# Flamingo layer with gated attention and experts, one core: the router's logits from the float16 halves, turned by DMA, instead of TensorE's float32 turns

## What is computed

```python
def reference(x, ctx_1024, g_xattn, g_ffn, ...):                # x and ctx: (8, 512, 512) float32
    x = x + tanh(g_xattn[0]) * xattn(layernorm(x), ctx, ctx, Wq, bq, Wk, bk, Wv, bv, Wo, bo)   # 16 heads of 32
    x = x + tanh(g_ffn[0]) * ffn(layernorm(x), Wr, br, W1, b1, W2, b2)

def ffn(x, Wr, br, W1, b1, W2, b2):
    probs = softmax(x @ Wr + br)            # the router: 4096 tokens, 8 experts
    gates, ids = top_k(probs, 2)
    # each expert takes up to 615 tokens, hidden size 2048, silu, and adds gate * result to its tokens
```

## Time and profile before

| | |
|---|---|
| time, median of 3 runs | 1811.75 us (1811.48 to 1812.64) |
| the profiled execution | 1810.6 us, of which the span is 1808.9 us |
| PE busy | 1727.7 us, 96% of the span |
| DVE, ACT, POOL busy | 60%, 44%, 24% |
| granted clock of PE, mean | 0.981 of full speed |
| attention | up to about 903 us of the span, 8 batches |

### The profile page before, as it was taken

How to read it: one execution, slowest core, us unless ns; L and a number is a source line. 1 busy time by engine, 2 the same in 40 slices (tenths; PEclk the granted TensorE clock), 3 DMA queues, 4 the chain that set the end, 5 groups by cost and what they waited for, 6 DMA issues and landing times.

```text
span 1808.9 us, 29536 instructions
## 1 busy us (share of the span) xinstructions
PE 1727.7 (96%) x10371; PEld 827.7 (46%) x10371; DVE 1076.8 (60%) x2087; ACT 798.2 (44%) x1093; POOL 434.4 (24%) x424
## 2 busy tenths in 40 slices
PE   6999999999999999999918999999999999999998
PEld 4324243342423334243305657475665647565563
DVE  6777867778776777867687625345252525434231
ACT  4553735547364554735423426153342516244240
POOL 2332434224343332431201211211021121112101
PEclk9999999999999999999958999999999999999999
DMA  6334263433425433243123542625263362626312
GB/s 227 106 86 125 71 167 113 102 119 100 144 93 142 137 93 116 81 114 109 42 100 105 133 124 100 168 87 154 71 174 80 120 148 88 179 50 177 75 44 29
DMA packets 214608, 203.19 MB, mean 112 GB/s; under 512 B 121813, under 2 KB 162913, under 8 KB 210457
## 3 DMA queue, kind: packets, MB, share of 16 engines
q1 hardware_dynamic: 193432, 181.80, 33.1%
q0 software_dynamic: 21120, 20.67, 6.6%
HBM read 134.57 MB, written 43.63 MB: 99 GB/s over the span
## 4 chain that ended last, share of the span: by engine, by line
PE 84%; DVE 10%; issue 3%; ACT 2%; POOL 1%; DMA 0%; SPq 0%; DVEq 0%; ACTq 0%; POOLq 0%
PE psum L1598 23%; PE psum L1574 21%; PE psum L1369 7%; PE psum L1376 6%; PE psum L1360 6%; PE psum L1350 6%; PE psum L1340 6%; PE psum L1462 5%; PE psum L1387 3%; DVE mx L938 2%; DVE reached L1092 1%; DVE x2hl L1012 1%; DVE x2hl L1014 1%; DVE stats L890 1%; DVE x2n L897 1%
## 5 line engine op out<-in xcount | busy, mean ns | idle before, releaser
L1598 PE MATMUL psum<-w,hT 128*128 128x512 f16 (+1 forms) x1920 | 415.7, 379 | 0.0
L1574 PE MATMUL psum<-xgT,w 128*128 128x308 f16 (+1 forms) x3072 | 408.1, 293 | 0.6 <-DVE xgT L1193 0.6
L938 DVE TENSOR_REDUCE mx<-psum 128x1 f32<-128x512 f32 x512 | 330.2, 683 | 104.1 <-PE psum L1350 102.5
L1574 PEld LDWEIGHTS psum<-xgT,w 128*128 128x128 f16 x3072 | 296.2, 97 | 109.3 <-DVE xgT L1193 1.1
L788 ACT ACTIVATE pt<-psum 128x1024 f32<-128x1024 f32 x256 | 255.0, 1022 | 116.4 <-PE psum L1360 116.4
L1598 PEld LDWEIGHTS psum<-w,hT 128*128 128x128 f16 (+1 forms) x1920 | 199.3, 104 | 213.8
L864 ACT ACTIVATE h<-psum,b1c 128x308 f32<-128x308 f32 (+1 forms) x256 | 117.9, 511 | 342.0 <-PE psum L1574 341.6
L1214 DVE TENSOR_TENSOR hT<-h,hT 128x615 f16<-128x615 f32 x128 | 102.5, 801 | 210.1 <-ACT hT L867 210.1
L681 POOL DMA_INDIRECT out_dram<-y,idx_now x40 | 87.6, 2191 | 498.8 <-DVE y L1246 305.8
L1243 DVE SCALAR_TENSOR_TENSOR y<-psum,b2b 128x512 f32<-128x512 f32 (+1 forms) x40 | 27.7, 691 | 269.4 <-PE psum L1598 269.4
L1340 PE MATMUL psum<-actT,wT 128*128 128x512 f16 x768 | 177.6, 379 | 2.0 <-DVE wT L925 2.0
(11 more groups left out here) (198 smaller groups left out, 1522.7 us busy)
## 6 DMA issues: line engine op xcount, KB each, us to landing
stage<-in_L_ffn_W_dram SPq DMA_DIRECT2D x62, 1024.0 KB, 5.9
stk<-qk_rows SPq DMA_DIRECT2D x192, 128.0 KB, 2.5
qk_rows<-qks SPq DMA_DIRECT2D x64, 256.0 KB, 2.5
xin<-in_x_dram SPq DMA_DIRECT2D x8, 1024.0 KB, 5.3
cin<-in_ctx_dram SPq DMA_DIRECT2D x8, 1024.0 KB, 7.5
xres<-in_x_dram SPq DMA_DIRECT2D x8, 1024.0 KB, 5.6
out_dram<-xres SPq DMA_DIRECT2D x32, 256.0 KB, 2.1
x_split<-x2hl SPq DMA_DIRECT2D x32, 256.0 KB, 2.3
```

The source lines that it names most:

```text
L938: v.reduce_max(mx[:, KT * t + qt:KT * t + qt + 1], ps, AX.X).then_inc(read, 1)
L1574: mm = t_.matmul(psum[:, (2 * m + ch) % 4, 0:c1 - c0], w1[:, wp, kt, m * P:(m + 1) * P], xgT[:, KT * xp + kt, c0:c1], start=(kt == 0 and ( ...
L1598: mm = t_.matmul(psum[0:rows, Y_BANK[i], :], hT[:, hp, k, c * P:c * P + rows], w2[:, wp, k, :], start=(k == 0 and (hp, wp) == (0, 0)), sto ...
```

## The change

The 16 transposes on PE in slot 2 and ACT's four copies of them are gone. SP turns `x2hl`, the halves that DVE has made already, by four DMA transposes of 128x1024 float16 into `x2T`, a float16 view of `x2nT`; they stand in SP's list behind `stack_heads` of tile 5 and ahead of the maxima of group 0, and only from batch 1 on. `wr` is split into halves once, ahead of the batches. `parts` is now three products for each quarter (high by high, high by low, low by high), 12 float16 products, in the second half of slot 5 ahead of that half's values, and PE waits there for all four transposes. `logits` moves to the second half of slot 6, behind that half's values.

```diff
-X2T_SLOT, PARTS_SLOT, LG_SLOT = 2, 4, 5
+PARTS_SLOT, LG_SLOT = 5, 6
...
+        wr_hl = sb("wr_hl", [P, 2, KT, 32], f16)
...
+        x2T = x2nT[:, :, :].rearrange("p k s -> p (k s)").bitcast(f16).rearrange("p (c s) -> p c s", s=S)
...
                 for i in range(QK_FIRST + 2):
                     stack_heads(sp, b, i)
+                if not first:
+                    sp.wait_ge(x2hl_ready, KT * b)
+                    settle(sp)
+                    for tt in range(KT):
+                        sp.dma_start(x2T[:, :, tt * P:(tt + 1) * P], x2hl[:, tt, :], transpose=True).then_inc(x2T_in, 16)
                 for g in range(NG):
 
                     sp.wait_ge(mrow_ready, NG * b + g + 1)
...
+            s.activation(wr_hl[:, 0, :, :], wr[:, :, :], ACT.Copy, scale=SW).then_inc(wr_hi, 1)
+
+            def logit_parts(b):
+                ps, read = filled(act, use, "lg_parts", b)
+                s.activation(lg_parts[:, :], ps, ACT.Copy, scale=1.0 / SW).then_inc(read, 1)
...
-                    if t == X2T_SLOT:
-                        rows()
                     if t == PARTS_SLOT:
-                        parts()
+                        logit_parts(b)
                     if t < LAG_B:
                         for tt in later_v(t):
                             values(tt)
                     if t == LG_SLOT:
-                        logits()
+                        logits(b)
...
+            dve.wait_ge(wr_hi, 1)
+            v.scalar_tensor_tensor(wr_hl[:, 1, :, :], wr[:, :, :], SW, wr_hl[:, 0, :, :], ALU.mult, ALU.subtract).then_inc(wr_split, 1)
...
+                    if first:
+                        pe.wait_ge(wr_split, 1)
+                    else:
+                        pe.wait_ge(x2T_in, 16 * KT * b)
+                    dst, full = claim(pe, use, "lg_parts", b)
+                    for xp, wp in PARTS:
+                        for kt in range(KT):
+                            last = t_.matmul(dst[32 * kt:32 * kt + 32, :], wr_hl[:, wp, kt, :], x2T[:, KT * xp + kt, :],
+                                             start=((xp, wp) == (0, 0)), stop=((xp, wp) == (1, 0)))
                     last.then_inc(full, 1)
...
-                    if s == X2T_SLOT:
-                        rows((2 * half, 2 * half + 1))
```

More of the change, by code:

```diff
@@ L251, in batch_banks @@
                     banks.add(("qk", i), (2, 4, 2, 4)[i - QK_FIRST])
-                if s == X2T_SLOT:
-                    for kt in range(KT):
-                        banks.add(("x2T", kt), (6, 7, 3, 5)[kt])
                 if s == PARTS_SLOT:
@@ L315, in layer_kernel @@
         settled = sem("settled")
-        wr_zero, pick_ready = sem("wr_zero"), sem("pick_ready")
+        wr_zero, wr_hi, wr_split, x2T_in, pick_ready = (
+            sem(n) for n in ("wr_zero", "wr_hi", "wr_split", "x2T_in", "pick_ready"))
         k_ones = sem("k_ones")
@@ L551, in _ @@
             g.memset(minus_half[:, :], -0.5).then_inc(consts_ready, 1)
-            g.memset(x2n[:, :, :], 0.0).then_inc(consts_ready, 1)
+            g.memset(x2nT[:, :, :], 0.0).then_inc(consts_ready, 1)
             pool.wait_ge(ident_zero, 1)
@@ L717, in _, with logits @@
             copied(act, pre, "bias")
[L719 to L734, removed]
+            s.activation(wr_hl[:, 0, :, :], wr[:, :, :], ACT.Copy, scale=SW).then_inc(wr_hi, 1)
+            def logit_parts(b):
+                ps, read = filled(act, use, "lg_parts", b)
+                s.activation(lg_parts[:, :], ps, ACT.Copy, scale=1.0 / SW).then_inc(read, 1)
+            def logits(b):
+                ps, read = filled(act, use, "lg", b)
+                settle(act)
+                s.activation(lg[:, b, :], ps[:, 0:KT * E], ACT.Copy).then_inc(read, 1)
             def batch(b, last):
-                rows, parts, logits = router_copy(use, b, b)
                 def queries_keys(i):
@@ L1295, in _, with batch @@
                 copied(pe, pre, ("w", 3, kt))
[L1297 to L1303, removed]
-                def parts():
[L1307 to L1312, removed]
+            def batch(b, last_batch, first=False):
+                def parts():
+                    if first:
[7 more added lines that the diff above has]
+                                             start=((xp, wp) == (0, 0)), stop=((xp, wp) == (1, 0)))
                     last.then_inc(full, 1)
                 def logits():
-                    copied(pe, where, "lg_parts", b)
-                    dst, full = claim(pe, where, "lg", b)
+                    copied(pe, use, "lg_parts", b)
+                    dst, full = claim(pe, use, "lg", b)
                     for tt in range(KT):
@@ L1322, in logits @@
                     last.then_inc(full, 1)
-                return rows, parts, logits
-            def batch(b, last_batch, first=False):
-                rows, parts, logits = router(use, b, KT * b)
                 def queries_keys(i, halves=range(2)):
@@ L1422, in batch @@
                         copied(pe, use, ("v", 2), b)
-                        copied(pe, use, ("x2T", 3), b)
                     if 0 <= u < UNITS and u % 4 == 0:
```

## The result

The changed kernel takes 1853.3 us (median of 4, 1852.5 to 1854.2) against 1811.6 us: a ratio of 1.023, with a 95% interval of 1.0217 to 1.0242. That is 41.7 us slower. The forecast had the direction, and 26.5 of these 42 us; the range ended at 1847.

What follows compares the result with a forecast made beforehand. It took DVE to set slots 2 to 4 and PE slot 5 and later; 3.43 us (3.08 + 0.35) for batches 1 to 7 and 2.53 for batch 0 made 26.5 us, so 1838 us, range 1828 to 1847.

Steps and rivals of the forecast that it cites:

- Slot 2: PE's transposes go, near 2 us a batch; DVE sets slots 2 to 4, so nothing comes through to slot 4.
- The 12 products: Slot 5: 12 float16 products take 0.8 us, between 0.65 side by side and 2.6 one after another.
- The wait for the transposes: Ahead of slot 5's 12 products PE waits 0.9 us (bounds 0.2 and 2.2), none in batch 0.
- theory A: From the experiments: ACT's order holds PE in slot 7, PE waits for DMA transposes, idling costs some 3 us of clock.
- What is queued behind on SP: Group 0's maxima issue from 495.4 to 498.1, in before 501, needed at 501.2; tiles 6 and 7 some 2.5 us later: hidden.
- The hold on ACT: Slot 7: exponentials queue behind the copy of `lg`; `with_values(0)` 3.08 us later, 0.81 moved products and 2.3 waiting.
- the sum: Batches 1 to 7 lose 3.43 us each, batch 0 2.53, together 26.5 us, giving 1838.
- The step that failed: Behind slot 7: the 3.08 us lateness of `with_values(0)` is not taken up, PE being full from there.
- the rivals: Later, 1847 or 1852, chance 0.07; below 1828, 0.06; faster, 1803, 0.04; within 0.2%, 0.03.
- the signs of being wrong: A batch shorter than 110 us, where 111.4 was forecast: ACT does not hold the exponentials, or slack behind slot 7.

Runs made afterwards that it cites:

- The bare replacement: Changed kernel with DMA transposes issued ahead of tile 4, products with `wr` back in slot 4 and logits back in slot 5: 1816.6 us.
- the kernel kept busy in both slots: Changed kernel plus products whose result nobody reads, 5 in slot 2 and 8 in slot 7: 1839.0 us.
- The early transposes: Changed kernel with the four DMA transposes issued ahead of tile 4 in place of behind tile 5: 1848.2 us.
- The two kernels kept busy: Changed kernel plus products whose result nobody reads, 8 in slot 7 alone (1839.3 us), or also 5 in slot 2 (1839.0 us).
- the filling of slot 2: The bare replacement plus 5 products in slot 2 whose result nobody reads: 1811.5 us.
- repacked: The bare replacement with PE's filling moved up, queries and keys in slots 0 to 3, values in slots 4 and 5: 1800.8 us.
- slot 7 kept busy: Changed kernel plus 8 products in slot 7 whose result nobody reads: 1839.3 us.
- the one with ACT's copy behind: Changed kernel with ACT's copy of the logits put behind the exponentials and the last values: 1824.7 us.

## Why the prediction was wrong

**Slot 2.** Right. PE waits for DVE (0.98, then four times 0.21 in slots 2 and 3), and slot 4 starts where it did, to 0.01 us. The prediction let 0.1 us through to slot 3 and nothing to slot 4; slot 3's extra work starts at 509.06, 486.88 in the time of before, where 486.9 was forecast. The bare replacement, which has the shorter products as well, gives 0.17 us a batch in all.

**The 12 products.** Right: 520.17 - 519.41 = 0.76 us, taken as 0.8.

**The wait for the transposes.** Right in its place, 0.7 to 1.0 us in batches 1 to 5 (forecast 0.9); in batch 6 PE came later, by a drop of its clock behind slot 2, and did not wait. Wrong for batch 7, where it was 1.72, and would have been more had not the same kind of drop made PE late: in the kernel kept busy in both slots it is 2.87. Counted from the start of the batch, PE is there at 34.88 us in place of 36.00 in batch 4, and the transfer lets it go at 37.75 in place of 36.76:

```profile
509.43 0.83 PE L1309 MATMUL psum<-x2nT,wr_hl 128*32 128x512 f16 x12 [0.76 <-DMA x2nT<-x2hl]
...
843.27 1.06 PE L1309 MATMUL psum<-x2nT,wr_hl 128*32 128x512 f16 x12 [2.87 <-DMA x2nT<-x2hl]
```

In batch 7 DVE has no statistics of a next input to make (the timeline has none), which fits PE's coming earlier; SP issued the four transposes 1.0 us later in the batch than would match, behind tile 5's reads, and why those are late was not followed. I had taken the batches as alike. It also shows that the parts of theory A do not quite add up: a drop of the clock ahead of a wait is in part covered by it.

**What is queued behind on SP.** Right: the maxima of group 0 were issued from 517.70 and PE did not wait for them in any batch. The early transposes showed no harm from tiles 4 and 5 being later.

**The hold on ACT.** Right in mechanism and near in size: 0.94 + 0.98 us of idle PE in slot 7, and from slot 0 of the batch to `with_values(0)` 3.12 us more than before (529.73 - 482.69 against 504.43 - 460.51), where 3.43 was forecast. Slot 6 began 0.16 us later than before (521.48 less 22.18, against 499.14), where 0.35 was forecast, and from there it was 8.25 us in place of the 8.37 of the sum.

**The step that failed** is the sentence at the end of that part, "It is not regained: from here PE is full". It takes what follows slot 7 at the durations of before, and so puts the clock's term at nothing without a reason. Of the 4.7 us a batch that the loop lost (585.01 - 472.32 = 112.7 against 108.0), 3.1 were there by `with_values(0)`; the other 1.6 came directly behind it (5.52 us in place of 3.94), mostly at half the clock, without any wait. The sum had no term for that, neither in the rivals nor in the range, and the signs of being wrong looked only for a batch shorter than forecast. The full clock of before (1.00 in both windows of the earlier trace rows) was taken over without a word into a kernel whose PE idles; it had been the clock of a PE that hardly idled. The two kernels kept busy measure the term: 14.3 us (1853.3 to 1839.0). With it the sum would be 1838 + 14 = 1852, and 1839.0 stands where 1838 was forecast. That closeness is in part luck, by errors that cancel: the loop's batches lost 3.0 in place of 3.4 us (110.97 against 108.0), batch 7 lost 6.3 (908.76 - 795.15 = 113.61 against 881.38 - 774.11 = 107.27, with a drop of the clock in it).

## What to carry to other kernels

When a change takes an engine's work out or lets it wait in a new place, list the waits and then ask of TensorE what clock it will have behind each; here two to five short waits in a row, 1.7 to 1.9 us together, were followed in many batches, though not in all, by a drop of the clock that cost 1.6 to 1.9 us on top of them (112.7 to 113.0 us a batch against 111.1, which is 108.0 and the 3.1 of waits). A small copy that has moved on the producer's side must be moved on the consumer's side too, or all that is queued behind it waits with it. And work taken from an engine is worth next to nothing in a stretch that another engine sets until the rest is packed into the hole: the same replacement was 5 us slower bare, even with the filling of slot 2, and 11 us faster repacked.

## What was not expected of the hardware

Products that nobody reads, put where TensorE would wait, made a kernel 14 us faster (1853.3 to 1839.3). Whether the clock drops behind a given hole is not settled by the hole: in one execution (the kernel before with its logits in slot 6) the same hold of 0.94 and 0.80 us was followed by a drop in batch 5 and by none in batch 4, in the changed kernel 0.84 and 0.95 us had one in batch 0 and none in batch 7; and with slot 7 kept busy a wait of 1.94 us had one in batch 1, one of 2.74 us none in batch 7. Which batches it hits varied from kernel to kernel; what decides it stays open. The first 48 products of batch 0 took 12.2 us in some profiled executions, again with the clock down, and 10.5 in others: 12.2 in the changed kernel and 10.5 in the one with ACT's copy behind, whose code is the same up to there. So these 1.7 us, which are in the profile of the changed kernel and not in that of before, are not the change's.
